# Rows of the sent experts in natural order, written with one 256 KB transfer per pair and copy, and two more banks for the last products

## The reference

```
x = x + tanh(g_xattn) * attention(layernorm(x), ctx)
x = x + tanh(g_ffn)   * ffn(layernorm(x))

ffn, with t = 32 positions per group, 32 experts e and 4 sets s, so 128 slots (e, s):
logits = grouped @ controller + tie                 # per group: 32 positions x 32 experts x 4 sets
perm   = (logits == max over positions)             # each slot picks one position
inner  = relu(f1[e, s] @ (picked row) + bias[e, s]) # 256 -> 32
y      = inner @ f2[e, s]                           # 32 -> 256
out    = rows of y put back to the positions that perm picked, and added
```

## Time and profile before

| | |
|---|---|
| median of 3 runs | 269.71 us |
| the profiled execution, by its own time | 269.4 us |
| its span in the profile | 267.7 us |
| mean granted TensorE clock | 0.973 |
| busy share of the span: PE, DVE, ACT, POOL | 82%, 75%, 62%, 48% |
| writes to y_rows (L401) | 32 of 128 KB |
| reads from y_rows (L412) | 8 of 512 KB |

### The profile page before, as it was taken

One profiled execution on the slowest core, in us unless ns is written; L12 is line 12 of the kernel. 1 busy time (PEld: TensorE's weight loads), 2 busy tenths in 40 slices (PEclk: granted clock), 3 DMA queues, 4 the chain that ended last, 5 costly groups with the idle time before them and its releaser, 6 DMA issues.

```text
span 267.7 us, 7540 instructions
## 1 busy us (share of the span) xinstructions
PE 219.2 (82%) x2850; PEld 171.6 (64%) x2850; DVE 200.1 (75%) x454; ACT 166.9 (62%) x356; POOL 129.1 (48%) x243
## 2 busy tenths in 40 slices
PE   0554776798887899898899998977998999994993
PEld 0444565576676688786677776756886777783551
DVE  3996747789999599596898886798698455553663
ACT  3633675768657778596677766435588544557571
POOL 5832175648746857777386869544466000000000
PEclk9995999999999999999999999998699999999999
DMA  7747479831435343325220000018993179799934
GB/s 221 206 105 197 127 221 237 229 104 50 132 103 142 93 113 95 98 62 140 63 61 4 7 4 6 2 33 320 389 384 138 40 175 247 193 232 220 200 136 140
DMA packets 32230, 37.91 MB, mean 142 GB/s; under 512 B 4099, under 2 KB 27331, under 8 KB 31939
## 3 DMA queue, kind: packets, MB, share of 16 engines
q1 hardware_dynamic: 31661, 36.82, 49.1%
q10 hardware_dynamic: 534, 0.61, 0.8%
HBM read 18.26 MB, written 6.29 MB: 92 GB/s over the span
## 4 chain that ended last, share of the span: by engine, by line
PE 32%; DVE 20%; POOL 16%; issue 13%; DMA 8%; ACT 6%; SPq 2%; ACTq 0%; POOLq 0%; DVEq 0%
POOL pT L481 6%; PE banks L856 4%; DVE rsum L1275 4%; PE banks L753 4%; PE banks L711 3%; PE banks L731 3%; PE banks L930 3%; DVE nmax L1267 3%; PE banks L874 3%; PE banks L915 3%; DMA y<-y_rows 2%; POOL xs L475 2%; ACT pT L1022 2%; PE banks L602 2%; DMA xs<-in_x_dram 2%
## 5 line engine op out<-in xcount | busy, mean ns | idle before, releaser
L481 POOL TENSOR_SCALAR_AFFINE_SELECT pT<-pT 128x512 f32<-128x512 f32 x64 | 40.8, 640 | 38.2 <-ACT pT L1022 38.2
L1267 DVE TENSOR_REDUCE nmax<-banks 128x4 f32<-128x512 f32 x64 | 43.7, 683 | 18.0 <-PE banks L665 17.6
L1027 ACT ACTIVATE banks<-cb 128x512 f32<-128x512 bf16 x62 | 37.1, 598 | 14.4 <-DVE nmax L1267 12.7
L1022 ACT ACTIVATE pT<-banks 128x512 f32<-128x512 f32 x64 | 37.6, 587 | 5.0 <-PE banks L682 4.9
L1275 DVE RECIPROCAL rsum<-banks 128x256 f32<-128x256 f32 x16 | 28.0, 1749 | 1.3 <-PE banks L711 1.3
L665 PE MATMUL banks<-kst,qst 96*128 96x128 bf16 x256 | 25.0, 220 | 3.3 <-ACT banks L1027 3.2
L711 PE MATMUL banks<-pT,va 128*32 128x128 f32 x512 | 27.3, 285 | 0.1
L711 PE MATMUL banks<-pT,ones 128*32 128x128 f32 x512 | 25.7, 273 | 0.0
L682 PE MATMUL banks<-qst,kst 99*128 99x128 bf16 x256 | 25.4, 222 | 0.3 <-ACT pT L1022 0.3
L1115 ACT ACTIVATE routed<-banks 128x512 f32<-128x512 f32 x30 | 17.2, 628 | 7.9 <-PE banks L753 7.9
L594 PE MATMUL banks<-cf,xn 128*128 128x128 f32 x32 | 6.0, 317 | 17.8 <-DVE xn L1220 15.1
(11 more groups left out here) (133 smaller groups left out, 622.1 us busy)
## 6 DMA issues: line engine op xcount, KB each, us to landing
wx<-in_wexp_dram SPq DMA_DIRECT2D x32, 256.5 KB, 6.7
kst<-kp SPq DMA_DIRECT2D x48, 128.0 KB, 2.6
qst<-qp SPq DMA_DIRECT2D x48, 128.0 KB, 2.4
cT<-in_ctxT_dram SPq DMA_DIRECT2D x8, 256.0 KB, 3.1
y_rows<-ring SPq DMA_DIRECT2D x16, 128.0 KB, 2.9
y<-y_rows SPq DMA_DIRECT2D x4, 512.0 KB, 5.4
wx<-y_rows SPq DMA_DIRECT2D x4, 512.0 KB, 8.6
out_dram<-xs SPq DMA_DIRECT2D x16, 128.0 KB, 2.0
```

The source lines that it names most:

```text
L481: pool.affine_select(p, p, [[0, HC], [1, P]], ALU.is_ge, 0.0, base=0, channel_multiplier=-1)\
L1022: act.activation(pT[:, n % PR, :], BT[n % 2], ACT.Exp, scale=float(D) ** -0.5).then_inc(p_ready, 1)
L1027: act.activation(BS[n % 2], causal, ACT.Copy).then_inc(mask_placed, 1)
L1267: dve.tensor_reduce(nmax[:, b % 2, :].rearrange("p (e j o) -> p e o j", e=2, o=KH)[:, e, o], BS[n % 2].rearrange("p (j t) -> p j t", j=HC) ...
```

## The change

- `SENT` is (0, 1, 2, 4, 5, 6, 8, 9) instead of (0, 1, 3, 4, 6, 7, 9, 10). The number of sent pairs stays eight.
- A sent pair now holds two neighbouring experts, and row i*4 + t*2 + c of `y_rows` is expert i, feature half t, parity c. So c and the group together make one run of DRAM, and a pair and a t go out in one transfer of 256 KB from 128 partitions: 16 writes instead of 32.
- A quarter is now 16 neighbouring rows, and it is read to 16 neighbouring partitions (64 to 79 for quarter 0, and so on) instead of to every fourth. Sizes and number of the reads stay.
- The reads stand at other places of SP's queue.
- `combine(12)` and `combine(13)` write into banks 6 and 7, which are free by then, and the waits for `yo_ready` from 12 on move accordingly.
- The columns of the controller follow the slots: three copies on POOL instead of four; the moving operand of `expert_in` for sent experts is addressed differently, with the same number of columns.

```diff
-SENT = (0, 1, 3, 4, 6, 7, 9, 10)
+SENT = (0, 1, 2, 4, 5, 6, 8, 9)
 KEPT = tuple(p for p in range(PAIRS) if p not in SENT)
...
+        by_copy_rows = y_rows.rearrange("(i t c) g j -> t (c g) i j", t=2, c=2)
...
-                    for c in range(2):
-                        at = (2 * c + t) * 16 + first
-                        sp.dma_start(y_rows[at:at + 9:8].rearrange("e g j -> g e j"),
-                                     sent[q % YR][t][c * HALF:(c + 1) * HALF].rearrange("g (e j) -> g e j", e=2))\
-                            .then_inc(y_sent[q % YR], 16)
+                    sp.dma_start(by_copy_rows[t, :, first:first + 2, :],
+                                 sent[q % YR][t].rearrange("p (e j) -> p e j", e=2)).then_inc(y_sent[q % YR], 16)
...
-                sp.dma_start((y0, yw)[late][HALF + quarter::4, :].rearrange("s (k x) -> s k x", k=2),
-                             y_rows[quarter::4].rearrange("s (k l x) j -> s k l (x j)", k=2, l=2)[:, :, late])\
+                rows = slice(quarter * 16, (quarter + 1) * 16)
+                sp.dma_start((y0, yw)[late][HALF + quarter * 16:HALF + (quarter + 1) * 16, :].rearrange("s (k x) -> s k x", k=2),
+                             y_rows[rows].rearrange("s (k l x) j -> s k l (x j)", k=2, l=2)[:, :, late])\
                     .then_inc(y_loaded[late], 16)
...
-                    pool.wait_ge(small_loaded, 16)
-                    for k in range(2):
-                        for c in range(2):
-                            at = (1 - k) * HALF + c * 32
-                            last = pool.tensor_copy(
...
+                    pool.tensor_copy(ctrl_sb[:, :, HALF:], ctrl_in[:, :, 0:HALF])
+                    for c in range(2):
+                        last = pool.tensor_copy(
...
-                                         routed[:, h, kind].rearrange("p k s x -> p (k s) x")[:, at + 16 * t::32, :],
+                                         routed[:, h, 1, :, 4 * at + 2 * t:4 * at + 2 * t + 2, :]
+                                         .rearrange("p k c x -> p k (c x)") if kind else
+                                         routed[:, h, 0].rearrange("p k s x -> p (k s) x")[:, at + 16 * t::32, :],
...
-            BC = bank[0:2]
+            BC = [bank[b % 2 if not 12 <= b < 14 else b - 6] for b in range(NB)]
...
-                if b >= 2:
+                if 2 <= b < 12:
                     pe.wait_ge(yo_ready, b - 1)
+                elif b >= 14:
+                    pe.wait_ge(yo_ready, b - 3)
```

More of the change, by code:

```diff
@@ L59 @@
 BIAS_SETS = 4
-SENT = (0, 1, 3, 4, 6, 7, 9, 10)
+SENT = (0, 1, 2, 4, 5, 6, 8, 9)
 KEPT = tuple(p for p in range(PAIRS) if p not in SENT)
-EXPERTS = tuple(e for p in range(PAIRS) for e in
-                ((SENT.index(p) // 2 + 4 * (SENT.index(p) % 2), SENT.index(p) // 2 + 4 * (SENT.index(p) % 2) + 8) if p in SENT
-                 else (PAIRS + 2 * KEPT.index(p), PAIRS + 2 * KEPT.index(p) + 1)))
+EXPERTS = tuple(2 * SENT.index(p) + i if p in SENT else PAIRS + 2 * KEPT.index(p) + i
+                for p in range(PAIRS) for i in range(2))
 YR = 4
@@ L398, in send_rows @@
                         sp.wait_ge(y_kept_dve, p + 1)
-                    for c in range(2):
-                        at = (2 * c + t) * 16 + first
-                        sp.dma_start(y_rows[at:at + 9:8].rearrange("e g j -> g e j"),
-                                     sent[q % YR][t][c * HALF:(c + 1) * HALF].rearrange("g (e j) -> g e j", e=2))\
-                            .then_inc(y_sent[q % YR], 16)
+                    sp.dma_start(by_copy_rows[t, :, first:first + 2, :],
+                                 sent[q % YR][t].rearrange("p (e j) -> p e j", e=2)).then_inc(y_sent[q % YR], 16)
             def load_rows(quarter, late):
                 for q in (2 * quarter, 2 * quarter + 1):
-                    sp.wait_ge(y_sent[q % YR], 4 * 16 * (q // YR + 1))
+                    sp.wait_ge(y_sent[q % YR], 2 * 16 * (q // YR + 1))
                 if late:
                     sp.wait_ge(e_done, PAIRS // 2)
-                sp.dma_start((y0, yw)[late][HALF + quarter::4, :].rearrange("s (k x) -> s k x", k=2),
-                             y_rows[quarter::4].rearrange("s (k l x) j -> s k l (x j)", k=2, l=2)[:, :, late])\
+                rows = slice(quarter * 16, (quarter + 1) * 16)
+                sp.dma_start((y0, yw)[late][HALF + quarter * 16:HALF + (quarter + 1) * 16, :].rearrange("s (k x) -> s k x", k=2),
+                             y_rows[rows].rearrange("s (k l x) j -> s k l (x j)", k=2, l=2)[:, :, late])\
                     .then_inc(y_loaded[late], 16)
-            send_rows(0)
-            send_rows(1)
-            send_rows(2)
+            for q in range(5):
+                send_rows(q)
             load_rows(0, 0)
-            send_rows(3)
-            send_rows(4)
+            send_rows(5)
             load_rows(1, 0)
-            send_rows(5)
             send_rows(6)
+            load_rows(0, 1)
+            send_rows(7)
+            load_rows(1, 1)
             load_rows(2, 0)
-            send_rows(7)
-            load_rows(0, 1)
             load_rows(3, 0)
-            for quarter in range(1, 4):
-                load_rows(quarter, 1)
+            load_rows(2, 1)
+            load_rows(3, 1)
             for b in range(NB):
@@ L929, in combine @@
                     at = k * YK + (b % (NB // 2) * 2 + i) * E
-                    last = pe.matmul(BC[b % 2][g * T:(g + 1) * T, 0:E],
+                    last = pe.matmul(BC[b][g * T:(g + 1) * T, 0:E],
                                      permT[:, b, g * T:(g + 1) * T],
@@ L1443, in keep_y @@
                     if q >= YR:
-                        dve.wait_ge(y_sent[q % YR], 4 * 16 * (q // YR))
+                        dve.wait_ge(y_sent[q % YR], 2 * 16 * (q // YR))
                     dve.tensor_copy(sent[q % YR][1], bank[5 + 2 * (p % 2)]).then_inc(y_kept_dve, 1)
@@ L1471, in _ @@
                 dve.wait_ge(c_done, b + 1)
-                dve.scalar_tensor_tensor(xs[:, b, :], bank[b % 2][:, 0:E], tg[:, 1:2], xs[:, b, :], ALU.mult, ALU.add)\
+                dve.scalar_tensor_tensor(xs[:, b, :], bank[b % 2 if not 12 <= b < 14 else b - 6][:, 0:E], tg[:, 1:2], xs[:, b, :], ALU.mult, ALU.add)\
                     .then_inc(yo_ready, 1)
```

6 lines of the change are left out of this document (3 added, 3 removed).

## The result

The changed kernel takes 276.51 us (median of 5 runs, 274.39 to 277.43) where the kernel before takes 269.71 (5 runs, 266.57 to 270.43). The ratio is 1.0366, with a 95% interval of 1.0305 to 1.0427: slower by 3.7%. The ratio leaves disturbed executions out; by the two medians it is 6.8 us, or 2.5%. The forecast was 284 us, range 270 to 289: the sign and the path through the queue of reads held, the reason given for the slow reads did not, and the size was too large by 7.5 us. The profiled execution took 276.51 us, span 274.8.

What follows compares the result with a forecast made beforehand. The prediction took the kernel to be bound by writes, then reads, then PE's combines. From 269.4 us it added 12.3 for `combine(0)` and 2.8 for the clock, less 0.5 for the banks: 284 us, range 270 to 289.

Steps and rivals of the forecast that it cites:

- the sign: Time of the whole kernel: slower by over 2%, given a chance of 0.73.
- the path through the queue of reads: Queued reads and writes keep the DMA engines busy, so the fourth read into `y0` delays `combine(0)` by 12.3 us.
- the reason given for the slow reads: Reads to 16 neighbouring partitions reach four blocks of four instead of sixteen, so each takes 4.9 us instead of 2.5.

Runs made afterwards that it cites:

- e3: The changed kernel with the four reads into `y0` queued ahead of all reads into `yw`: 278.67 us, ratio 1.0294 to the kernel before.
- e10: The changed kernel with its last four reads reordered, so that queue neighbours twice go to the same 16 partitions: 283.48 us, ratio 1.0551 to the kernel before.
- e4: The kernel before with only the two more banks for `combine(12)` and `combine(13)`: 268.53 us, ratio 0.9977.
- e7: The kernel before with only the other sent pairs, the last being pair 9 instead of 10: 268.02 us, ratio 0.998.

## What to carry to other kernels

Before a transfer to few partitions is made "simpler", look at which partitions it touches: here sixteen neighbours took 1.8 times as long as sixteen that take all values of bits 4 to 2 of their number, and a step of two or four cost nothing. It is to be had wherever the order of slots can be chosen freely, as here by the columns of a weight matrix. Price a queue of transfers by how long each holds the engines, and look for everyone who takes from it, the second half of the combines and the engines' own instructions too. When stretches ahead of a change scatter by microseconds, measure from the start of the stretch that the change touches.

## What the runs showed of the hardware that was not expected

- The engines' instructions share the DMA engines with the data: with long packed reads queued, a packet of instructions came 8 to 9 us later than in the kernel before (26.8 to 27.5 against 18.4 us) and PE stopped for 2.5 to 3.3 us, in all five traces that have full-size packed reads and the joined writes (the changed kernel and e3's order, twice each, and e10), with the reservation above on the cause.
- Eight blocks of partitions are served about as fast as sixteen (200 and 213 GB/s, a read every 2.5 us in both), and four ports give 117 to 126 GB/s, some 30 GB/s a port, more than half of what eight give.
- The low clock after an idle moves with the idle: e3 took the wait from c(0) to c(8) and paid the slow combines there. Waits of 2.99 us (e4) and 3.76 us (e7) were followed by it, one of 2.81 us (before) was not.
